# Reordering three engines of a normalise-and-convolve kernel: C copied ahead of high B, plane D ahead of low B, root ahead of variance, a first half-plane made earlier, and another order of the tail

## The reference

```python
def _quantize(weight, Wp, Wn):
    max_val = jnp.max(jnp.abs(weight))
    w_norm = weight / max_val
    delta = 0.05 * jnp.max(jnp.abs(w_norm))
    tern = jnp.where(w_norm > delta, 1.0, jnp.where(w_norm < -delta, -1.0, 0.0))
    return jnp.where(tern > 0, Wp[0] * tern, jnp.where(tern < 0, Wn[0] * tern, tern))

def _gn(v, G=32, eps=1e-05):
    g = v.reshape(B_, G, C_ // G, H_, W_)
    m, s = jnp.mean(g, axis=(2, 3, 4), keepdims=True), jnp.var(g, axis=(2, 3, 4), keepdims=True)
    return ((g - m) / jnp.sqrt(s + eps)).reshape(v.shape)

x = x + conv3x3(_gn(x), _quantize(weight, Wp, Wn)) + bias   # padding 1, NCHW
```

## Time and profile before

| | us |
|---|---|
| median of three runs (lowest to highest) | 546.74 (545.43 to 547.09) |
| time of the profiled execution | 545.59 |
| its span | 543.8 |
| busy PE, DVE, ACT, POOL | 521.0, 525.8, 476.0, 151.3 |

### The profile page before, as it was taken

One profiled execution on the slowest core, in us unless ns is written; L12 is line 12 of the kernel. 1 busy time (PEld: TensorE's weight loads), 2 busy tenths in 40 slices (PEclk: granted clock), 3 DMA queues, 4 the chain that ended last, 5 costly groups with the idle time before them and its releaser, 6 DMA issues. The chain is left out here.

```text
span 543.8 us, 8599 instructions
## 1 busy us (share of the span) xinstructions
PE 521.0 (96%) x3174; PEld 305.5 (56%) x3174; DVE 525.8 (97%) x446; ACT 476.0 (88%) x485; POOL 151.3 (28%) x138
## 2 busy tenths in 40 slices
PE   1989999999999999999999999999999999999994
PEld 0555555555555555555555555555555555555552
DVE  4999999999999999999999999999999999999895
ACT  2999999999999999999999999999999999999870
POOL 3113323322323322232332232332223233223220
PEclk9999999999999999999999999999999999999998
DMA  8538999999999999999999999999999999998766
GB/s 291 227 117 219 307 292 291 286 269 276 321 268 374 255 310 314 286 310 282 345 276 290 331 247 374 237 348 300 277 268 374 261 335 272 289 297 213 184 186 251
DMA packets 27985, 152.96 MB, mean 281 GB/s; under 512 B 3488, under 2 KB 3488, under 8 KB 27936
## 3 DMA queue, kind: packets, MB, share of 16 engines
q1 hardware_dynamic: 18576, 102.77, 48.4%
q0 software_dynamic: 8784, 48.98, 45.9%
q10 hardware_dynamic: 576, 0.59, 0.3%
HBM read 100.94 MB, written 51.38 MB: 280 GB/s over the span
## 5 line engine op out<-in xcount | busy, mean ns | idle before, releaser
L809 PE MATMUL odd_rows<-parts,w_lhsT 128*128 128x392 f16 (+1 forms) x1536 | 262.5, 326 | 0.1
L809 PE MATMUL even_rows<-parts,w_lhsT 128*128 128x392 f16 (+1 forms) x1536 | 262.3, 326 | 0.2 <-DVE parts L657 0.2
L809 PEld LDWEIGHTS odd_rows<-parts,w_lhsT 128*128 128x128 f16 x1536 | 149.0, 97 | 103.1 <-DVE parts L650 0.5
L809 PEld LDWEIGHTS even_rows<-parts,w_lhsT 128*128 128x128 f16 x1536 | 147.0, 98 | 106.3 <-issue 10.4
L650 DVE SCALAR_TENSOR_TENSOR parts<-plane,norm_scale,parts 128x1568 f16<-128x1568 f32 x111 | 204.6, 1855 | 1.1 <-ACT parts L430 1.1
L342 POOL TENSOR_TENSOR plane<-x 128x756 f32<-128x756 f32 x64 | 94.1, 1470 | 350.6 <-DVE plane L622 211.6
L430 ACT ACTIVATE parts<-plane,norm_scale 128x1568 f16<-128x1568 f32 x111 | 175.5, 1594 | 16.8 <-DVE norm_scale L640 9.4
L469 ACT ACTIVATE junk<-x,negmean 128x3136 f16<-128x3136 f32 x32 | 92.6, 2894 | 0.0
L371 POOL DMA_DIRECT2D y<-in_x_dram x61 | 54.3, 1031 | 23.0 <-DVE y L667 21.6
L667 DVE SCALAR_TENSOR_TENSOR y<-odd_rows,out_scale,c_sb 128x1568 f32<-128x1568 f32 x31 | 57.2, 1845 | 0.0
L667 DVE SCALAR_TENSOR_TENSOR y<-even_rows,out_scale,d_sb 128x1568 f32<-128x1568 f32 x31 | 57.2, 1845 | 0.0
(11 more groups left out here) (67 smaller groups left out, 133.7 us busy)
## 6 DMA issues: line engine op xcount, KB each, us to landing
x<-in_x_dram SPq DMA_DIRECT2D x64, 784.0 KB, 13.1
out_dram<-y SPq DMA_DIRECT2D x63, 784.0 KB, 7.3
y<-in_x_dram POOLq DMA_DIRECT2D x61, 784.0 KB, 12.8
out_dram<-y SPq DMA_DIRECT2D x2, 392.0 KB, 5.5
y<-in_L_conv_weight_dram ACTq DMA_DIRECT2D x1, 576.0 KB, 6.4
wp_sb<-in_L_conv_Wp_dram ACTq DMA_DIRECT2D x1, 0.5 KB, 7.5
wn_sb<-in_L_conv_Wn_dram ACTq DMA_DIRECT2D x1, 0.5 KB, 7.7
bias_sb<-in_L_conv_bias_dram ACTq DMA_DIRECT2D x1, 0.5 KB, 7.6
```

What stands on the lines that cost most here:

```text
L809: ins = nc.tensor.matmul(product_ps(odd, b, b + 1)[:, 0, r0 - b * BANK_ROWS:r1 - b * BANK_ROWS, :], w_lhsT[:, prod, kh, :], part(img, prod ...
```

## The change

In ACT's `root`, `std` is written first and `neg_var` second, and PE waits for the second of them where it waited for `std`. In ACT's slots that have a next image, `copy_c(now)` stands ahead of `make_hi(now, B)`. In DVE's slots, `make_d(nxt)` and `first_rstd(nxt)` stand ahead of `make_lo(now, B)`. For the first image, POOL makes the first half of plane B as soon as the first half of x is there, and DVE makes the second half, after low D (`make_last_rows_of_b`). In the last slot, DVE adds x to both halves of `c_sb` and then to both halves of `d_sb`, ahead of all outputs.

```diff
         half_x_loaded = sem("half_x_loaded")
+        half_b_ready = sem("half_b_ready")
         half_hi_ready = sem("half_hi_ready")
...
                         ins.then_inc(plane_ready[B], 1)
+                    elif img.j == 0:
+                        ins.then_inc(half_b_ready, 1)
 
                 def first_half_b(img, now):
-                    pool.wait_ge(x_loaded[img.buf], img.turn * 32 + 32)
                     wait(pool, lo_ready[B], img.count())
                     if now:
+                        pool.wait_ge(x_loaded[img.buf], img.turn * 32 + 32)
                         wait(pool, product_done[A], now.half(1, 1, 1))
...
                     else:
-                        pool.wait_ge(sum_ready, img.count(plus=1))
+                        pool.wait_ge(half_x_loaded, 16 * (p + 1))
                     difference_b(img, 0)
...
                 def second_half_b(img, prev):
-                    if prev:
-                        wait(pool, product_done[B], prev.half(1, 1, 1))
+                    wait(pool, product_done[B], prev.half(1, 1, 1))
                     pool.wait_ge(lo_ready[D], img.count(plus=1))
...
                 def emit(prev, now, nxt, far):
-                    if now:
+                    if prev and now:
                         second_half_b(now, prev)
...
                     b = b_slice(img)
+                    nc.scalar.activation(std[:, b], var_ps, ACT.Sqrt, bias=eps_sb[:],
+                                         scale=-VAR_SCALE).then_inc(std_ready, 1)
                     nc.scalar.activation(neg_var[:, b], var_ps, ACT.Identity, bias=neg_eps_sb[:],
                                          scale=VAR_SCALE).then_inc(var_ready, 1)
-                    nc.scalar.activation(std[:, b], var_ps, ACT.Sqrt, bias=eps_sb[:],
-                                         scale=-VAR_SCALE).then_inc(std_ready, 1)
 
...
                             sum_squares(nxt)
-                        make_hi(now, B)
-                        copy_c(now)
                         if nxt:
+                            copy_c(now)
+                            make_hi(now, B)
                             root(nxt)
+                        else:
+                            make_hi(now, B)
+                            copy_c(now)
                         if far:
...
 
+                def make_last_rows_of_b(img):
+                    dve.wait_ge(half_b_ready, p + 1)
+                    even = columns(x_sb[img.buf], EVEN)
+                    nc.vector.tensor_tensor(plane[B][:, ROWS:, 0:PAIRS - 1], even[:, ROWS:, 0:PAIRS - 1], even[:, ROWS:, 1:],
+                                            ALU.subtract).then_inc(plane_ready[B], 1)
+
                 def make_a(img):
...
 
-                def make_first_lo(img):
-                    for h, hi, lo in ((0, half_hi_ready, half_lo_ready), (1, hi_ready[C], lo_ready[C])):
-                        dve.wait_ge(hi, p + 1 if h == 0 else img.count(plus=1))
-                        nc.vector.scalar_tensor_tensor(first_rows(part(img, C, LO), h), first_rows(plane_of(img, C), h),
-                                                       norm_scale[:, b_slice(img)], first_rows(part(img, C, HI), h),
-                                                       ALU.mult, ALU.subtract).then_inc(lo, 1)
+                def make_first_lo(img, h):
+                    hi, lo = ((half_hi_ready, half_lo_ready), (hi_ready[C], lo_ready[C]))[h]
+                    dve.wait_ge(hi, img.count(plus=1) if h else p + 1)
+                    nc.vector.scalar_tensor_tensor(first_rows(part(img, C, LO), h), first_rows(plane_of(img, C), h),
+                                                   norm_scale[:, b_slice(img)], first_rows(part(img, C, HI), h),
+                                                   ALU.mult, ALU.subtract).then_inc(lo, 1)
 
...
                         dve.wait_ge(product_done[prod], img.half(b1 // 2 - 1, 1, 1))
-                    dve.wait_ge(last_residual, 4 * p + 2 * (b0 // 2) + odd + 1)
+                    dve.wait_ge(last_residual, 4 * p + b0 // 2 + (1 if odd else 3))
                     wait(dve, y_stored[img.buf][b0 // 2], img.turn * 16)
...
                         make_first_d(nxt, 1)
-                        make_first_lo(nxt)
+                        make_first_lo(nxt, 0)
+                        make_first_lo(nxt, 1)
                     elif now:
...
                             output_rows(prev, ODD)
-                        if second_slot and p == 0:
-                            output_scales()
+                        if second_slot:
+                            make_last_rows_of_b(now)
+                            if p == 0:
+                                output_scales()
                         make_lo(now, A)
...
                             make_c(far)
-                        if second_slot:
+                        if nxt:
                             make_d(nxt)
+                            first_rstd(nxt)
                         make_lo(now, B)
                         if nxt:
-                            first_rstd(nxt)
-                            if not second_slot:
-                                make_d(nxt)
                             newton_factor(nxt)
...
                                 add_half_residual(prev)
-                            for odd in (EVEN, ODD):
-                                add_last_residual(now, 0, odd)
+                            for odd in (ODD, EVEN):
+                                for h in range(HALVES):
+                                    add_last_residual(now, h, odd)
                             last_output_rows(now, 0, 2, EVEN, first_rows_done[EVEN])
                             last_output_rows(now, 0, 2, ODD, first_rows_done[ODD])
-                            for odd in (EVEN, ODD):
-                                add_last_residual(now, 1, odd)
                             last_output_rows(now, 2, 3, EVEN, last_rows_done[EVEN])
...
                         turn_weights((D, A, B))
-                        pe.wait_ge(std_ready, nxt.count(plus=1))
+                        pe.wait_ge(var_ready, nxt.count(plus=1))
                         sum_second_mean(far)
...
                             multiply(now, A, 2)
-                            pe.wait_ge(std_ready, nxt.count(plus=1))
+                            pe.wait_ge(var_ready, nxt.count(plus=1))
                             if far:
```

## The result

The changed kernel takes 540.34 us in the median of four runs (539.95 to 540.36). The kernel before, timed beside it, has 546.09 (544.97 to 547.09). The ratio is 0.989 with an interval of 0.9868 to 0.9912: 5 to 7 us faster, 6.0 in the middle. The forecast was 542.3, 2.0 us too high, at a gain of 4.4 where the medians show 5.75.

What follows compares the result with a forecast made beforehand. The prediction took a ring through `std` to set the 16.05 us slot, DVE's sum just under it. Slots 3.6, start 0.8 and tail 0 make 4.4 us off the median 546.74: 542.3 us, range 540.2 to 545.2.

Steps and rivals of the forecast that it cites:

- The ring through `std`: Middle slots: low C, PE's C and D, variance, `std`, reciprocal, next low C; sets 16.05 us now, 15.94 after.
- DVE's own sum: Middle slots: DVE's work without its 0.14 us wait at the reciprocal, 16.05 - 0.14 = 15.91 us a slot.
- The ring through product A: Middle slots: C to product A, even output, low C and PE's next C; 15.88 to 15.97, taken as 15.92 us.
- The fourth limit: Middle slots: PE waits for C's copy before the statistics; copying earlier takes 0 to 0.07 us off two limits, counted nothing.
- The moves costed at nothing: Middle slots: later high B and low B delay no reader, with covers of 0.8 us at low B, 1.7 at product B.
- The start: First image's plane B: 0.5 us at PE's first product plus 0.25 to 0.3 in its slot; together 0.8 (0 to 1.2).
- The copy of C before high B lets PE go on earlier there too, but DVE sets that slot: First image's slot: the earlier copy lets PE resume sooner, but DVE sets the slot's length; no separate gain given.
- From the profiled execution to the median: Whole run: the profiled 545.59 us gives 541.2; it lay 1.15 below the median 546.74, so the forecast is 542.3.
- The tail: Last slot: DVE's last output up to 0.8 us earlier, but stores drain 3.2 MB in 7.8 us; counted 0.
- Rival B: ACT, middle slots: C's copy waits for product C, `std` comes 0.2 us late; slot 16.15, 548.9 us; chance 4%.
- C (transfers): x loads: the transfers hold the shorter slot; if they held half the gain, 544.5 us; chance 4%.
- Rival A: Middle slots: even output really waits for product A, slot stays 16.05, only the start gains; 545.9 us; chance 12%.

## Why the prediction was right or wrong

- **What sets the slot: right.** The ring through `std` and DVE's sum just under it were read from one long pitch; std first alone and std first undone show it from both sides, and the last slot, where DVE has less to do and waits, is as long as the others.
- **DVE's own sum, 15.91: right** (15.908). The ring through product A, 15.92 with 0.04 for the handing over: 15.89, the 0.04 right; A begins 8.00 after C and not 8.04, for the early copy of C.
- **The fourth limit, counted at nothing: mis-sized.** C's early copy takes 0.04 from the ring (8.22 to 8.18), so the ring is 15.90, not 15.94, and the slot 15.91, not 15.93. 4.3 us instead of 3.6. Without the early copy the slot is 15.945 and 1.1 us in the run are gone.
- **The moves costed at nothing: right as covers.** Low B never waits for high B in the changed kernel; without plane D ahead it does, for 25 us. Product B never waits for low B in the slots.
- **The start: right in size for the profiled execution** (0.90 instead of 0.8), by the rows named: `w_neg` 0.88, low A 1.83, and PE's first product 0.54 earlier (20.27 to 19.73) where 0.5 was taken. Alone it is not worth that, for a stop that the profile doesn't explain.
- **"The copy of C before high B lets PE go on earlier there too, but DVE sets that slot": the step that failed.** It weighed PE's wait of 1.75 us by the chain only. In about half of the executions of the kernel before (28 of 61) it cost the clock, and then PE, not DVE, set that slot: product A took 5.78 us and the even output waited 1.55 for it. A second profile would have been needed to see it; the three times, 545.43 to 547.09, were the hint.
- **From the profiled execution to the median: failed with it.** The sum gave 541.2 for an execution like the profiled one, and 539.95 to 540.36 came: 0.8 to 1.2 short. The 1.15 added to reach the median was carried over as if it were scatter. By the two groups it was the half-level clock, which the change removes, and so the forecast came out a further 1.15 too high. That is the larger part of the 2.0 us; the slots are 0.7 of it and the start 0.1. Like against like, the lower group of the kernel before (median 545.3) against 540.34, the change gains 5.0, close to the 4.3 of the slots and 0.9 of the start.
- **The range, 540.2 to 545.2: met at its low end, and by luck.** The low end was built from 5.1 for the slots and 1.2 for the start. They gave 4.3 and 0.9, and the clock, which the range didn't have in it, filled the room.
- **The tail, 0: right**, and its reason, the drain, was shown by moving the drain. In the profiles the stretch from image 30's even output to the end is 27.5 us before and 27.0 after, but the runs with and without the new order don't differ, so these 0.5 us are not shown to be the order's.
- **Rival B (late `std`) and C (transfers):** neither came. ACT's idle time before `std` is 0.43 in the changed kernel, close to the cover of 0.4 read ahead. x loads take 13.9 us in the median and plane C waits for none in the slots. Rival A, the slot at 16.05, is out by the slot itself.

## What to carry to other kernels

A wait of a tenth of a microsecond that a saturated engine has in each iteration shows in no busy share; compare the pitch of each instruction with that of its kind, and follow the ring that closes there, with every other ring priced beside it. An edit that is free beside another can be ruinous alone (C's copy first: +25 us), so test parts in the order in which their covers are put in place. And when a kernel's times fall into two groups, find the place before explaining a median: here one idle stretch of PE, and one instruction moved once.

## What the hardware showed unexpectedly

- A wait of 1.6 to 1.75 us of PE, after eight us of dense work, is followed in about half of the executions by a fall of its granted clock from 1.00 to 0.50 for some 3 us; waits of 0.20 to 0.90 never were, in 55 runs. The Trainium skill, page "TensorE: Matmul & The Clock Gate", section "What's actually happening", has the two levels, 1.2 and 2.4 GHz, and idleness as what brings the lower one. The trace agrees on both (0.50 and 1.00 after a wait of 1.74); the page asks for a longer idle stretch than that, and there the measurement decides.
- DVE stood still for 0.33 to 0.34 us ahead of plane D in the slot of the second image in the two kernels with the start's edits and the old slot, and in no other; the profile gives no releaser. Open.
- From PE's recorded end to DVE's start pass 0.04 us, from ACT's `std` to DVE 0.03.
